# Attention probabilities split before the transpose: one transposing DMA per head pair in place of ten TensorE transposes

## The reference, cut to what matters

```python
scores = jnp.einsum('bsghd,btgd->bghst', q, k) * scale
p = jax.nn.softmax(scores, axis=-1)
return jnp.einsum('bghst,btgd->bsghd', p, v)
...
core = _gqa(q, k, v).reshape(b, s, nh * d)      # 256 own keys
xout = _gqa(qx, kx, vx).reshape(b, s, nh * d)   # 64 context keys
cat = jnp.concatenate([core, xout], axis=-1)
catq = _div_clamp_fp8(cat, proj_smooth)
return jnp.einsum('bsi,oi->bso', catq, wproj) * (proj_in_scale * proj_w_scale)
```

## Time and profile before

| | |
|---|---|
| median of 3 runs | 1147.81 us (1147.45 to 1148.67) |
| span of the profiled execution | 1146.5 us |
| PE busy | 1045.5 us (91%) |
| DVE busy | 916.7 us (80%) |
| ACT busy | 766.1 us (67%) |
| POOL busy | 698.6 us (61%) |
| DMA | 21.45 MB, mean 19 GB/s |

### The profile page before, as it was taken

One profiled execution on the slowest core, in us unless ns is written; L12 is line 12 of the kernel. 1 busy time (PEld: TensorE's weight loads), 2 busy tenths in 40 slices (PEclk: granted clock), 3 DMA queues, 4 the chain that ended last, 5 costly groups with the idle time before them and its releaser, 6 DMA issues.

```text
span 1146.5 us, 22682 instructions
## 1 busy us (share of the span) xinstructions
PE 1045.5 (91%) x7648; PEld 751.5 (66%) x7648; DVE 916.7 (80%) x1807; ACT 766.1 (67%) x2441; POOL 698.6 (61%) x533
## 2 busy tenths in 40 slices
PE   1567999998999999899899989999999999999998
PEld 0355677776776777677677767777776556555554
DVE  8898899998998999899899989998999683333332
ACT  2466878877887888788788878778877542222222
POOL 4776777677676857776586767777674242222222
PEclk9867899999999999999999999999999999999999
DMA  9321000000000000000000000000002110000000
GB/s 257 95 74 37 1 2 2 1 2 1 0 0 1 0 0 0 1 0 0 1 0 0 0 1 0 0 1 0 0 19 67 55 52 20 1 17 2 0 18 18
DMA packets 17409, 21.45 MB, mean 19 GB/s; under 512 B 1360, under 2 KB 15024, under 8 KB 17344
## 3 DMA queue, kind: packets, MB, share of 16 engines
q1 hardware_dynamic: 13232, 18.67, 5.1%
q0 software_dynamic: 4112, 2.10, 1.3%
HBM read 20.76 MB, written 2.10 MB: 20 GB/s over the span
## 4 chain that ended last, share of the span: by engine, by line
DVE 51%; issue 20%; PE 12%; ACT 12%; POOL 4%; DVEq 0%; DMA 0%; ACTq 0%; POOLq 0%
DVE nmx L1001 8%; DVE yb L1058 8%; DVE pT L1010 6%; DVE ss L1033 5%; POOL pT L1410 4%; ACT raw L700 4%; DVE var L1044 3%; DVE ss L1042 3%; ACT prob L741 3%; ACT yb L759 2%; DVE qT L1027 2%; ACT sq L699 2%; DVE stage L966 2%; DVE yb L1055 2%; PE S L351 2%
## 5 line engine op out<-in xcount | busy, mean ns | idle before, releaser
L1320 POOL TENSOR_TENSOR rstd<-var,mhalf 128x8 f32<-128x8 f32 (+1 forms) x128 | 176.5, 1379 | 205.4 <-DVE var L1037 202.1
L314 PE MATMUL A<-w_hi,xq 128*128 128x256 f16 (+1 forms) x1024 | 186.7, 251 | 39.9 <-ACT raw L700 21.5
L1372 POOL TENSOR_TENSOR raw<-raw,rstd 128x1024 f32<-128x1024 f32 (+1 forms) x128 | 185.9, 1452 | 10.0
L741 ACT ACTIVATE prob<-S,nmx 128x256 f32<-128x256 f32 x256 | 119.0, 470 | 107.4 <-DVE nmx L1001 107.3
L315 PE MATMUL A<-w_lo,xq 128*128 128x256 f16 (+1 forms) x1024 | 182.9, 251 | 0.0
L1410 POOL TENSOR_TENSOR pT<-zq,pT 128x512 f16<-128x512 f32 (+1 forms) x56 | 65.2, 1166 | 172.8 <-ACT pT L843 164.5
L314 PEld LDWEIGHTS A<-w_hi,xq 128*128 128x128 f16 x1024 | 101.9, 100 | 63.9 <-ACT raw L700 24.8
L848 ACT ACTIVATE qT<-A 128x512 f32<-128x512 f32 (+1 forms) x56 | 33.4, 596 | 146.4 <-PE A L308 146.3
L1360 POOL TENSOR_TENSOR prob<-prob,rl 128x1024 f32<-128x1024 f32 x64 | 121.2, 1893 | 16.2 <-DVE rl L1050 16.2
L341 PE MATMUL S<-kT,qT 128*128 128x256 f32 x512 | 122.5, 382 | 1.3 <-ACT kT L721 1.0
L1001 DVE TENSOR_REDUCE nmx<-S 128x2 f32<-128x512 f32 (+1 forms) x192 | 114.1, 595 | 8.1 <-PE S L351 8.1
(11 more groups left out here) (190 smaller groups left out, 2828.5 us busy)
## 6 DMA issues: line engine op xcount, KB each, us to landing
stage<-wallT SPq DMA_DIRECT2D x8, 1024.0 KB, 4.9
wp<-wpT POOLq DMA_DIRECT2D x1, 2048.0 KB, 30.6
out<-v_lo SPq DMA_DIRECT2D x8, 256.0 KB, 2.2
xs<-x SPq DMA_DIRECT2D x1, 1792.0 KB, 20.9
sq<-w2s SPq DMA_DIRECT2D x7, 128.0 KB, 3.0
sq<-w1T SPq DMA_DIRECT2D x3, 256.0 KB, 2.8
sq<-w3T SPq DMA_DIRECT2D x3, 256.0 KB, 3.1
raw<-w1T SPq DMA_DIRECT2D x3, 256.0 KB, 2.8
```

The costliest lines, as they stand in the source:

```text
L314: nc.tensor.matmul(o, l, w_hi[:, c, col:col + n], start=(c == 0), stop=False)
L741: last = nc.scalar.activation(prob[:, p, j, :], o[:, t * S:(t + 1) * S], ACT.Exp, bias=nmx[:, p, j:j + 1], accum_out=lsum[:, p, j:j + 1])
L1320: return nc.gpsimd.tensor_tensor(dst, src, mhalf[:, 0:n], ALU.pow)
L1372: nc.gpsimd.tensor_tensor(raw[:, p, u, :], raw[:, p, u, :], rstd[:, p, u].rearrange("p (u o) -> p u o", o=1).to_broadcast([P, w, D]), ALU. ...
```

## The change

- The probabilities are split while they still have tokens on the 128 rows. `high_p` is now one ACT copy of prob (128x1024, 4-byte to 16-bit, SBUF to SBUF) and one of probx (128x256); `low_p` is two DVE subtractions of the same sizes with both inputs in SBUF. They write psrc, 128 x 2560 numbers of 16 bits.
- One DMA per step, issued by SP (`flip`, dma_start_transpose), transposes psrc into pT: 20 blocks of 128x128. It waits for low_p of this step and for the cross product of step n-2. The ten TensorE transposes of a step are gone.
- high_p comes behind read_q(0) on ACT, in place of scale_out; low_p comes as one piece behind variances_q on DVE. Before, both were in three pieces, most of them later in the tick. PE waits for the DMA in pv_core of the next tick.
- The cross product has high and low halves stacked on 128 rows: two matmuls of 512 columns in its own bank XB (T1 before) instead of six of 256. The transposes of q, cross q and k all go through T0. The transposed z and zf go to XB; they stand between transpose_q(0) and project_q(1) on PE, and front_ln and tail_high stand between high_p and read_q(1) on ACT, in ticks 2 and 6. tail_low comes before squares_q.
- The factor 1024 that was in high_p and low_p is now in `sums`: one more DVE tensor_scalar of 128x8, and a wait for it.
- The DMA scratch of POOL's queue is set to 8192.

```diff
+            def flip(n, p):
+                done(sp, d_pl, n)
+                done(sp, mm_xo, n - 2)
+                sp.dma_start_transpose(pT[:, p, :, :], psrc[:, p, :]).then_inc(ld_pT[p], 16)
...
                 def pv_core(n, p, vg):
-                    done(pe, d_p0, n); done(pe, d_p1, n)
-                    done(pe, a_xo, n - 1)
+                    pe.wait_ge(ld_pT[p], (b * (G // 2) + (g - 4) // 2 + 1) * 16)
+                    done(pe, a_core, n - 1)
...
+                def pv_cross(n, p, vg):
+
+                    done(pe, a_xo, n - 1)
+                    both = pT[:, p, PX0:PX0 + PJ, :].rearrange("p j s -> p (j s)")
+                    nc.tensor.matmul(XB[:, :], vx_hi[:, vg, :], both, start=True, stop=False)
+                    nc.tensor.matmul(XB[:, :], vx_lo[0:SC, vg, :], both[0:SC], start=False, stop=True).then_inc(mm_xo, 1)
...
                 if live(n0): project_q(n0, 0)
-                if live(n0 - 5): pv_cross(n0 - 5, par(5), (g - 5) % G, 1)
                 if live(n0 - 1): transpose_q(n0 - 1, par(1), 0)
+                if g == FRONT_G and live(n0):
+                    done(pe, fr_z2, b + 1)
+                    done(pe, a_xo, n0 - 5)
+                    transpose_tokens(z, fr_T)
+                if g == TAIL_G and live(n0) and live(b - 1, B):
+                    done(pe, ta_z, b - 1)
+                    done(pe, a_xo, n0 - 5)
+                    transpose_tokens(zf, ta_T)
+                if live(n0): project_q(n0, 1)
                 if live(n0 - 1): transpose_q(n0 - 1, par(1), 1)
-                if live(n0): project_q(n0, 1)
                 if live(n0): project_kv(n0)
-                if live(n0 - 3): transpose_p(n0 - 3, par(3), 0)
+                if live(n0 - 4): pv_core(n0 - 4, par(4), (g - 4) % G)
                 if live(n0): project_x(n0)
                 if live(n0 - 1): transpose_k(n0 - 1, par(1))
                 if live(n0 - 2): scores_cross(n0 - 2, par(2))
-                if live(n0 - 4): pv_core(n0 - 4, par(4), (g - 4) % G)
-                if live(n0 - 3): transpose_p(n0 - 3, par(3), 1)
-                if live(n0 - 3): transpose_px(n0 - 3, par(3))
...
+                def high_p(n, p, half):
+
+                    done(act, g_norm, n)
+                    if live(n - 2):
+                        act.wait_ge(ld_pT[p], half * 16)
+                    nc.scalar.activation(psrc[:, p, 0:PSELF], prob[:, p, :, :, :].rearrange("p k j s -> p (k j s)"), ACT.Copy)
+                    nc.scalar.activation(pair(p)[:, :, 0, :], probx[:, p, :, :], ACT.Copy).then_inc(a_ph, 1)
...
                 if live(n0): read_q(n0, par(0), 0)
-                if live(n0 - 5): scale_out(n0 - 5, par(5), 1, (g - 5) % G)
+                if live(n0 - 3): high_p(n0 - 3, par(3), b * (G // 2) + (g - 3) // 2)
+                if g == FRONT_G and live(n0):
+                    front_ln(b + 1)
+                if g == TAIL_G and live(n0) and live(b - 1, B):
+                    tail_high(b - 1)
                 if live(n0): read_q(n0, par(0), 1)
...
+                def low_p(n, p):
+                    done(dve, a_ph, n)
+                    nc.vector.tensor_tensor(psrc[:, p, PSELF:2 * PSELF], prob[:, p, :, :, :].rearrange("p k j s -> p (k j s)"),
+                                            psrc[:, p, 0:PSELF], ALU.subtract)
+                    nc.vector.tensor_tensor(pair(p)[:, :, 1, :], probx[:, p, :, :], pair(p)[:, :, 0, :], ALU.subtract
+                                            ).then_inc(d_pl, 1)
...
+                    nc.vector.tensor_scalar(lsum[:, p, :], lsum[:, p, :], 1.0 / PSCALE, None, ALU.mult).then_inc(d_ls, 1)
+                    done(dve, d_ls, n)
                     nc.vector.reciprocal(rl[:, p, :], lsum[:, p, :]).then_inc(d_rl, 1)
...
                 if live(n0): variances_q(n0, par(0))
-                if live(n0 - 3): low_p(n0 - 3, par(3), 0)
+                if live(n0 - 3): low_p(n0 - 3, par(3))
...
-                if live(n0 - 3): low_p(n0 - 3, par(3), 2)
                 if live(n0 - 1): maxima(n0 - 1, par(1), 0)
-                if live(n0 - 3): low_p(n0 - 3, par(3), 1)
                 if live(n0 - 1): maxima(n0 - 1, par(1), 1)
```

More of the change, by code:

```diff
@@ L277, in _ @@
             assert 2 * HC * UW <= NU * D
+            for n in range(STEPS - G, STEPS - 4):
+                flip(n, n % 2)
             sp.wait_ge(d_ss, STEPS - 1)
             load_up(0)
+            flip(STEPS - 4, 0)
             sp.wait_ge(mm_kT, STEPS - 1)
@@ L408, in transpose_k @@
-                    nc.tensor.transpose(T1[:, S:KT], raw[0:SC, p, UKX, :], idt[0:SC, 0:SC]).then_inc(mm_kT, 1)
-                def transpose_p(n, p, k):
-                    o, s = (T0, mm_p0) if k == 0 else (T1, mm_p1)
-                    if k == 0:
-                        done(pe, g_norm, n)
-                        if live(n + 2):
-                            done(pe, d_qxT, n + 2)
-                        else:
-                            done(pe, d_px, n - 1)
-                    elif live(n + 2):
-                        done(pe, a_kT, n + 2)
-                    else:
-                        done(pe, d_p1, n - 1)
-                    for j in range(HPG * ST):
-                        last = nc.tensor.transpose(o[:, j * P:(j + 1) * P], prob[:, p, j, k * P:(k + 1) * P], idt[:, :])
-                    last.then_inc(s, 1)
@@ L426, in transpose_px @@
-                def transpose_px(n, p):
-                    done(pe, d_p0, n)
-                    for h in range(HPG):
-                        both = probx[:, p, h * ST:(h + 1) * ST, :].rearrange("p t c -> p (t c)")
-                        last = nc.tensor.transpose(T0[:, h * P:(h + 1) * P], both, idt[:, :])
-                    last.then_inc(mm_px, 1)
+                        nc.tensor.transpose(T0[:, t * P:(t + 1) * P], raw[:, p, UK + t, :], idt[:, :])
+                    nc.tensor.transpose(T0[:, S:KT], raw[0:SC, p, UKX, :], idt[0:SC, 0:SC]).then_inc(mm_kT, 1)
@@ L806, in tick @@
                 if live(n0 - 2): exp_cross(n0 - 2, par(2))
-                if live(n0 - 4): scale_out(n0 - 4, par(4), 0, (g - 4) % G)
-                if live(n0 - 3): high_p(n0 - 3, par(3), 2)
-                if live(n0 - 3): high_p(n0 - 3, par(3), 1)
-                if g == FRONT_G and live(n0):
-                    front_ln(b + 1)
-                if g == TAIL_G and live(n0) and live(b - 1, B):
-                    tail_high(b - 1)
+                if live(n0 - 4): scale_out(n0 - 4, par(4), 1, (g - 4) % G)
                 for k in preps[-1:]:
@@ L1085, in tick @@
                     if g == 1:
+                        low_p(n0 - 3, par(3))
                         ffn_tick(0, 0)
-                        for k in (0, 2, 1): low_p(n0 - 3, par(3), k)
                         best(0, 0, NT - ST, 1)
-                        for k in range(2): low_p(n0 - 2, par(2), k)
+                        low_p(n0 - 2, par(2))
                         ffn_low(1)
@@ L1092, in tick @@
                     if g == 2:
-                        low_p(n0 - 3, par(3), 2)
                         ffn_tick(0, 1)
@@ L1411, in ffn_tick @@
                                         ).then_inc(f_alo, 1)
-            tick(B, 0)
-            tick(B, 1)
+            for g in range(2):
+                tick(B, g)
             exps(0, 0, NT - ST)
```

211 lines of the change are left out of this document (90 added, 121 removed).

## The result

The changed kernel takes 1303.3 us in the median (1297.8 to 1305.0), the kernel before 1148.2 us: a ratio of 1.134, 95% interval 1.132 to 1.137. That is 155 us slower; 106 were forecast, the range of 1190 to 1320 holds it.

What follows compares the result with a forecast made beforehand. It took a DVE and ACT loop of 12.34 us per tick as today's bound. New ticks 57 x 13.4 = 764, turns 13, ticks 2 and 6 46, against 726.84: +96, with +5 and +5 +106, 1254 us; range 1190 to 1320.

Steps and rivals of the forecast that it cites:

- the 0.95 charged: POOL's L1320 waits for DVE's new 128x1024 subtraction: 0.95 us per tick, bounds nothing and 1.4.
- rival 1: POOL's L1320 isn't held out and keeps its 1.63 us; tick 12.5, time 1203 us; chance 0.2.
- the 10.5 us forecast: Free time behind low_p that hides the transposing DMA; beyond it each microsecond costs half a microsecond per tick.
- the turn of the loop: Seven loop turns between ticks 6 and 63, each 1.9 us beyond a tick, 13 us together.
- PE's relief: PE loses some 1.6 us of work per tick, which by itself buys nothing but makes room for new waits.
- rival 4: Faster: PE is the bound after all and its 1.6 us less shorten the tick; 1056 us at full price; chance 0.1.
- Loop B closes: ACT's high_p, ahead of read_q(1), waits for POOL's g_norm, closing a loop of 12.4 us, 13.4 with the hold-out.
- is no loop yet: In the kernel before, nobody needs POOL's g_norm early, so its 8.15 us chain from L1320 closes no loop.
- eight plain ticks: Plain attention ticks, forecast at 13.4 us each: POOL's loop of 12.45 plus 0.95 of hold-out.
- stalls of ticks 2 and 6: Token transposes before project_q(1), front_ln and tail_high before read_q(1): 3.5 and 3.0 us lost, 46 us in all.
- Rival 3: TensorE's clock falls as PE is less dense: some 1 us more per tick, about 1310 us; chance 0.08.
- DVE's relief: Moving low_p frees about 1.0 us on DVE; if nothing else moved, last maxima come 0.4 to 0.7 us sooner.

Runs made afterwards that it cites:

- x3_swap: Changed kernel with DVE's two low_p subtractions in the other order, 128x256 first and 128x1024 behind it; 1259.2 us.
- x4_late: Changed kernel with the transposing DMA held back until the next step's first maxima are done, about 5.4 us after low_p; 1305.6 us.
- x8_later: Changed kernel with the transposing DMA held back until DVE has read the next step's self query, about 9.3 us after low_p; 1435.8 us.
- x12_unswap: 128x1024 subtraction first again, in the kernel with tokens moved, cross query in XB, copy behind read_q(1) and 128x256 first; 1163.5 us against 1115.1.
- x1: Changed kernel with token transposes of ticks 2 and 6 behind PE's self scores, front_ln and tail_high behind ACT's second scale_out; 1231.6 us.

## Why the prediction was right, and where it was not

**Right.** The sign and its main reasons: the subtraction with two SBUF inputs holds POOL out, 2.55 us where 2.58 follow from the 0.95 charged, and x3_swap prices it at 44 us (0.8 per tick); rival 1, that POOL isn't held out, is refuted. No row before had this case: in rows 10 POOL came first and DVE waited, and in rows 9 DVE's instruction reads one tensor of SBUF, not two, so rows 9 don't show the rule for two inputs that they were quoted for. The DMA is hidden: 4.9 us, inside 3.1 to 9.6, and no wait of PE in pv_core; in x4_late and x8_later its room is near the 10.5 us forecast. The first ticks (5 forecast, 4.6 measured) and the turn of the loop (1.9, 1.64) were close; the end cost 8 instead of 5. PE's relief bought nothing, as said, since PE wasn't the bound: rival 4 fell.

**The step that failed in kind: "Loop B closes".** The sum let the hold-out reach the tick through ACT, whose copy would wait for g_norm. ACT doesn't wait (0.6 us in 26 ticks), and the prediction named that as what would make it wrong in kind. It was close: in the batch shown POOL's probx ends 0.11 to 0.32 us before the copy starts, in every tick but the turn of the loop. The reading of before at fault is the sentence that POOL's chain "is no loop yet". It was one, though 0.26 us short of the bound: DVE's front work already ended 1.2 us behind POOL's prob, and the row of L920, read there only as DVE holding POOL, shows both directions: it starts at 527.26, POOL's prob ended at 528.15, and L920 ends 0.55 later; after, the same instruction (605.71, 1.95 us) ends 0.56 behind POOL's prob. The price of the hold-out came out right because it lies in POOL's chain either way, and the tick came out near because three loops of nearly the same length stand side by side; that is luck. x12_unswap tells the ways apart: with ACT's way cut, the order still costs 48 us.

**A step that was missing: the shared bank.** The diff lets the cross query wait for DVE's read of the self query (done(pe, d_qT, n)); the prediction didn't list this added wait. It costs DVE 0.75 us and ends a wait of 0.26 for ACT: 0.50 in the tick shown. Alone with x1 it is worth 16 us, without ACT's copy 26.

**Terms that were mis-sized.** For one batch:

| term | forecast | measured |
|---|---|---|
| eight plain ticks | 8 x 13.4 = 107.2 | 8 x 13.9 = 111.2 |
| stalls of ticks 2 and 6 | 3.5 + 3.0 = 6.5 | 4.98 + 5.28 = 10.3 |
| turn of the loop, and what plain ticks differ from 13.9 | 1.9 | 1.6 - 0.2 = 1.4 |
| sum | 115.6 | 122.9 |

The plain tick is 0.5 short, in ticks 2 to 5 as much as the bank adds. For the stalls, read_q(1) starts 5.83 us after g_norm (566.65, behind the end of POOL's probx at 560.82), where 4.8 were forecast: project_q(1), queued behind the token transposes, was left out, and both ran at half the clock. From there to POOL's next power instruction it is 4.06 us (566.65 to 570.71), where 2.89 were forecast: DVE's second read_q, whose transposes stand behind project_q(1), and low_v's wait of 0.62 were left out as well. Rival 3 (the clock falls) was thus true in these two ticks of eight (granted clock 0.82 in both) and at the turn of the loop (0.89), and in none of the other five (1.00); it was given as an alternative to the forecast, and came with it. Both errors point the same way: 7 x 7.3 = 51 us, about the 49 by which the forecast is short.

**DVE's relief.** It was to reach its last maxima 0.4 to 0.7 us sooner. It reached their end later (7.5 against 7.0 us after its variances), because freed time in front of a hold is no time: the hold ends with POOL's raw, wherever DVE's own work ends, and raw itself ends 0.7 later (4.55 against 3.82 us after the power instruction's start).

The change isn't bound to be slow. With the tokens out of the way, the copy behind read_q(1), the short subtraction first and the cross query in the other bank, the same idea runs in 1115.1 us, and with the factor folded in 1109.0 (ratio 0.965, 0.962 to 0.968).
